# A four-engine selective-scan kernel: front steps in another order, folded kept blocks, and late sums moved behind products

## The chip, the cores and the metric

One Trainium2 chip, one core. The time is that of the device, in microseconds (us), for one launch of the whole program. TensorE is called PE in the profile, VectorE DVE, ScalarE ACT, GpSimd POOL, SyncE SP.

## The reference, cut to what matters

Four layers work on an image of 4 x 64 x 64 x 64 (batch, channels, height, width). Layer 1 is the one that the change touches. It runs the block below twice, over the columns and over the rows of the image, with 256 sequences of 64 steps each time.

```python
def selective_scan(u, delta, A, B, C, D):
    A = jnp.clip(A, -5.0, 5.0)
    dA = jnp.einsum('bld,dn->bldn', delta, A)
    dB_u = jnp.einsum('bld,bld,bln->bldn', delta, u, B)
    c = jnp.concatenate([dA[:, 1:], jnp.zeros_like(dA[:, :1])], axis=1)
    c = jnp.flip(c, axis=1)
    c = jnp.cumsum(c, axis=1)
    c = jnp.exp(jnp.minimum(c, 15.0))
    c = jnp.flip(c, axis=1)
    x = jnp.cumsum(dB_u * c, axis=1) / (c + 1e-06)
    y = jnp.einsum('bldn,bln->bld', x, C)
    return y + u * D

def mamba(x, in_w, conv_w, conv_b, xproj_w, dproj_w, dproj_b, A_log, Dp, out_w):
    x1, res = jnp.split(x @ in_w.T, 2, axis=-1)
    ...
    x1 = jax.nn.silu(jnp.transpose(xc, (0, 2, 1)))
    x_dbl = x1 @ xproj_w.T
    delta = jax.nn.softplus(x_dbl[..., :DTR] @ dproj_w.T + dproj_b)
    B = x_dbl[..., DTR:DTR + N]
    C = x_dbl[..., DTR + N:]
    y = selective_scan(x1, delta, A, B, C, Dp)
    return y * jax.nn.silu(res) @ out_w.T
```

The inner width d is 192 and there are 96 states n. So the scan is 96 times a cumulative sum over the steps, for each of 192 channels, and a weighted sum of all of them.

## The kernel before, in words

`build` runs six phases one after the other. The third and fourth are `phase_axis`, once with `vertical=True` (tiles with the prefix `h_`) and once without (`w_`). The other phases are not touched.

**Bodies.** `phase_axis` works on 64 bodies T, each of four sequences of 64 steps: two groups g, of two sequences each, whose 128 steps lie on the partitions in the scan. `bodies` gives every engine the same order of bodies, the first and the last few unrolled and the rest in a loop. Five instruction streams are written out by hand, one per engine, and meet at semaphores. Each engine takes its own stream strictly in order.

**Pairs and chunks.** The 96 states of both groups make 96 pairs P of states per body; 8 pairs are a chunk, so a body has 12 chunks. For a chunk:

- TensorE makes the exponents, three groups j of them (`fill`, into the PSUM tile `pe_e`), the third of a chunk at its predecessor's pairs 2 and 3.
- ScalarE turns each group into the factor c (`c_group`, into `cbuf`) and the weighted ratio 1/(c + 1e-6) (`r_group`, into `rbuf`), both as sigmoids. `cbuf` and `rbuf` have two halves, so a chunk's first group waits until the pairs of two chunks before are used up.
- The product of c and dx = delta * x is made by VectorE (`product`, into `xr`, 3 deep), with B folded in, in two instructions. For some pairs it is made without B: by POOL in place in `cbuf` (the list `OTHER`, 35 pairs), or by VectorE in one instruction (`WIDE`, 13 pairs). For these 48 pairs ScalarE makes a triangle scaled by B for each state (`triangles`, into `tb`, a ring of 6), 96 of them per body.
- TensorE multiplies by the triangle, which is the cumulative sum (`sums`, into `pz`, two banks), two pairs ahead.
- VectorE weights the result with C and the ratio (`weighted`).

**The sum over states.** Two pairs are a unit U (48 per body, 24 per group). `weighted` puts each unit in one of four places. The first kept unit of a group goes into `sm`, the other kept ones into `wr` (3 deep), and POOL adds them to `sm` (`add`). The first sent block of two units goes into `held` (8 slots, that is two halves of 4), the others into `sent` (2 deep), from where POOL issues a transfer that accumulates into `held` (`send`, 768 KB). At the end of a group POOL adds both halves of `held` to `sm` (`add_held`) and folds `sm` into `yb` (`tree`), at U = 34 for group 0 and U = 47, the last, for group 1 (`TREE_AT`). In POOL's stream the products of a unit stand before its additions, and the held additions and the tree stand after them.

**The front.** Between the pairs each engine does a step of the next body's front, and of the last body's end, all through one PSUM tile `pf`, whose uses are in a fixed order that `s_ff` (full) and `s_fe` (free) count: Y (y of the body before, turned), O (output projection), X (input projection and convolution), DT (step size), BC (B and C), Z (gate). Tables such as `X_SLOTS` say after which pair TensorE issues which matmul; ScalarE and VectorE take theirs at fixed chunks and pairs (`sig_x`, `parts`, `log`, `bc_copy`, `sig_z`, `piece1`, `piece2`, `out`; `make_xc` at pair 31, `prefix` at 54, `make_gate` at 58, `gated` at 12). `log` needs a table load before its logarithm and one after it. SP stores the suffix sum's three bf16 pieces and loads them in another layout (`feed`); TensorE waits for them at pair 84.

## Time and profile before

| | us |
|---|---|
| median of 3 runs | 18634.21 (18628.9 to 18642.46) |
| the profiled execution, its own time | 18637.84 |
| its span | 18636.1 |
| TensorE busy (matmuls) | 15693.2 (84%) |
| VectorE busy | 15893.3 (85%) |
| ScalarE busy | 15051.5 (81%) |
| POOL busy | 14571.3 (78%) |
| mean granted TensorE clock | 0.955 |

Busy time is the time in which an engine executes. A row of a timeline has the start, the length, the engine, the line, the tiles and the count of like instructions merged into it, and in brackets the idle time of the engine ahead of it and what ended it. Times are counted from the start of the span. A row of busy time by windows has the window, its length, then busy time (and count of instructions) of PE, PEld (its weight loads), DVE, ACT and POOL, the granted TensorE clock (1.00 is full speed), the share of the 16 DMA engines, and GB/s.

### The profile page before, as it was taken

To read this page: it belongs to the slowest core of one execution; us is meant where nothing else is said; L and a number is where in the kernel's file an instruction comes from. 1 tells how busy PE (TensorE), PEld (TensorE's weight loads), DVE (VectorE), ACT (ScalarE), POOL (GpSimd) and SP (SyncE) were. 2 spreads that over 40 slices of the span, in tenths; PEclk is the share of its full clock that TensorE was granted. 3 is DMA by queue.
4 is the path that set the end of the run, shared out by engine and by line. 5 is a ranking of instruction groups with operands and counts; after the bars stand their busy time and mean duration, and the time that the engine had idled before them with its cause. 6 is when DMAs were issued, how large, how long until landed. Compare 5 with 4: busy or idle time off the path is not lost. (4 is left out here: it accounts for less than half of the span.)

```text
span 18636.1 us, 316924 instructions
## 1 busy us (share of the span) xinstructions
PE 15693.2 (84%) x72568; PEld 10136.5 (54%) x72568; DVE 15893.3 (85%) x42315; ACT 15051.5 (81%) x26177; POOL 14571.3 (78%) x11848
## 2 busy tenths in 40 slices
PE   8878888888888888888788888888888888887788
PEld 3335555555555556555455555555555566654233
DVE  7998888888888888888888888888888888887799
ACT  7768888888888888888788888888888888885488
POOL 4668888888888888888688888888888888886577
PEclk9999999999999999999899999999999999999899
DMA  2013443444434444344344344444344443443000
GB/s 40 16 24 68 69 71 66 69 69 69 71 67 69 68 70 70 66 70 69 59 69 72 67 71 68 69 73 69 68 70 69 71 71 67 71 69 62 22 15 15
DMA packets 1109721, 1150.84 MB, mean 62 GB/s; under 512 B 915424, under 2 KB 934524, under 8 KB 1107836
## 3 DMA queue, kind: packets, MB, share of 16 engines
q0 software_dynamic: 165888, 906.04, 25.2%
q1 hardware_dynamic: 938596, 221.43, 10.6%
q8 instruction: 707, 11.58, 0.3%
q14 instruction: 1178, 9.65, 0.2%
q10 hardware_dynamic: 3352, 2.14, 0.1%
HBM read 152.05 MB, written 71.35 MB: 12 GB/s over the span
## 5 line engine op out<-in xcount | busy, mean ns | idle before, releaser
L1356 ACT ACTIVATE h_cbuf<-h_pe_e 128x1024 f32<-128x1024 f32 x2304 | 2361.0, 1025 | 1240.0 <-PE h_pz L1685 746.4
L1356 ACT ACTIVATE w_cbuf<-w_pe_e 128x1024 f32<-128x1024 f32 x2304 | 2360.9, 1025 | 1234.6 <-PE w_pz L1685 750.0
L1517 POOL TENSOR_TENSOR h_cbuf<-h_cbuf,h_dxs 128x384 f32<-128x384 f32 x2240 | 2500.6, 1121 | 1004.1 <-ACT h_cbuf L1356 967.9
L1517 POOL TENSOR_TENSOR w_cbuf<-w_cbuf,w_dxs 128x384 f32<-128x384 f32 x2240 | 2465.9, 1106 | 945.2 <-ACT w_cbuf L1356 899.5
L1495 POOL TENSOR_TENSOR h_sm<-h_sm,h_wr 128x768 f32<-128x768 f32 x1536 | 2951.8, 1922 | 294.2 <-DVE h_wr L1230 203.0
L1495 POOL TENSOR_TENSOR w_sm<-w_sm,w_wr 128x768 f32<-128x768 f32 x1536 | 2936.5, 1912 | 255.7 <-DVE w_wr L1230 200.9
L1689 PE MATMUL h_pz<-h_xr,h_tri 128*128 128x384 f32 x6144 | 2769.2, 533 | 427.2 <-DVE h_sent L1230 228.4
L1689 PE MATMUL w_pz<-w_xr,w_tri 128*128 128x384 f32 x6144 | 2764.6, 532 | 403.4 <-DVE w_sent L1230 227.0
L1230 DVE SCALAR_TENSOR_TENSOR h_wr<-h_pz,h_bct,h_rbuf 128x192 f32<-128x192 f32 x6144 | 2225.0, 410 | 511.0 <-PE h_pz L1685 325.4
L1230 DVE SCALAR_TENSOR_TENSOR w_wr<-w_pz,w_bct,w_rbuf 128x192 f32<-128x192 f32 x6144 | 2225.2, 410 | 472.9 <-PE w_pz L1685 330.6
L1685 PE MATMUL w_pz<-w_cbuf,w_tb 128*128 128x192 f32 x8960 | 1988.1, 347 | 498.1 <-POOL w_cbuf L1517 290.4
L1379 ACT ACTIVATE h_rbuf<-h_pe_e 128x1024 f32<-128x1024 f32 x2304 | 2364.7, 1026 | 37.0 <-DVE h_wr L1230 33.1
L1379 ACT ACTIVATE w_rbuf<-w_pe_e 128x1024 f32<-128x1024 f32 x2304 | 2364.8, 1026 | 35.1 <-DVE w_wr L1230 30.9
L1685 PE MATMUL h_pz<-h_cbuf,h_tb 128*128 128x192 f32 x8960 | 1982.2, 346 | 485.7 <-POOL h_cbuf L1517 264.8
L1178 DVE SCALAR_TENSOR_TENSOR w_xr<-w_cbuf,w_bct,w_pdx 128x192 f32<-128x192 f32 x6144 | 2239.0, 405 | 114.4 <-ACT w_cbuf L1356 102.9
L1178 DVE SCALAR_TENSOR_TENSOR h_xr<-h_cbuf,h_bct,h_pdx 128x192 f32<-128x192 f32 x6144 | 2238.7, 405 | 110.9 <-ACT h_cbuf L1356 101.2
L1371 ACT ACTIVATE w_tb<-w_tri,w_bct 128x128 f32<-128x128 f32 x6144 | 2052.8, 406 | 0.0
L1371 ACT ACTIVATE h_tb<-h_tri,h_bct 128x128 f32<-128x128 f32 x6144 | 2052.3, 406 | 0.0
L1668 PE MATMUL h_pe_e<-h_decay,h_lt 128*128 128x256 bf16 x9216 | 1828.0, 281 | 142.3 <-ACT h_rbuf L1379 89.0
L1668 PE MATMUL w_pe_e<-w_decay,w_lt 128*128 128x256 bf16 x9216 | 1827.5, 281 | 123.1 <-ACT w_rbuf L1379 89.0
L1685 PEld LDWEIGHTS w_pz<-w_cbuf,w_tb 128*128 128x128 f32 x8960 | 1500.6, 201 | 771.0 <-issue 543.3
L1685 PEld LDWEIGHTS h_pz<-h_cbuf,h_tb 128*128 128x128 f32 x8960 | 1494.9, 200 | 761.3 <-issue 532.7
(381 smaller groups left out, 30563.3 us busy)
## 6 DMA issues: line engine op xcount, KB each, us to landing
h_held<-h_sent POOLq DMA_DIRECT2D x576, 768.0 KB, 5.8
w_held<-w_sent POOLq DMA_DIRECT2D x576, 768.0 KB, 5.8
h_lt<-pieces_s SPq DMA_DIRECT2D x512, 96.0 KB, 6.4
w_lt<-pieces_s SPq DMA_DIRECT2D x512, 96.0 KB, 7.3
pieces_s<-h_pieces SPq DMA_DIRECT2D x384, 48.0 KB, 2.1
pieces_s<-w_pieces SPq DMA_DIRECT2D x384, 48.0 KB, 2.1
h_xt<-first_s SPq DMA_DIRECT2D x34, 128.0 KB, 9.0
w_xt<-first_s SPq DMA_DIRECT2D x34, 128.0 KB, 7.4
```

What stands on the lines that cost most here:

```text
L1178: ins = v.scalar_tensor_tensor(xr[:, P % 3, m * DX:(m + 1) * DX], cbuf[:, ch % 2, (n + m) % 16, :], bct[:, par, g * 2 * NX + n + m:g * 2 * ...
L1230: ins = v.scalar_tensor_tensor(place(g, u, (P % 2) * 2 + m), pz[:, P % 2, m * DX:(m + 1) * DX], bct[:, par, g * 2 * NX + NX + n + m:g * 2 ...
L1356: a.activation(cbuf[:, ch % 2, :, 64 * j:64 * j + 64].rearrange("p n (b d) -> p b n d", b=2), pe_e[:, G % 2 * 2:G % 2 * 2 + 2, :].rearrang ...
L1371: ins = a.activation(tb[:, i % RING, m, :], tri[:], ACT.Copy, scale=bct[:, q, g * 2 * NX + n + m:g * 2 * NX + n + m + 1])
L1379: a.activation(rbuf[:, ch % 2, :, 64 * j:64 * j + 64].rearrange("p n (b d) -> p b n d", b=2), pe_e[:, G % 2 * 2:G % 2 * 2 + 2, :].rearrang ...
L1495: tt(sm[:, g], sm[:, g], wr[:, RINGED.index((g, u)) % 3], ALU.add).then_inc(s_add, 1)
L1517: tt(c2, c2, dxs[:, g:g + 1, :].broadcast_to([128, 2, DX]), ALU.mult).then_inc(s_xo, 1)
L1668: mm = t.matmul(dst, lt[:, par, g * JQ + m, :], decay[:, m, n0:n0 + 16, :], start=True, stop=True)
L1685: mm = t.matmul(pz[:, P % 2, m * DX:(m + 1) * DX], tb[:, i % RING, m, :], x[:, m * DX:(m + 1) * DX], start=True, stop=True)
L1689: t.matmul(pz[:, P % 2, 0:2 * DX], tri[:], x, start=True, stop=True).then_inc(s_z, 1)
```

## The change

It does these things, in both axis phases:

- The uses of `pf` in a body come as X, DT, BC, Y, O, Z instead of Y, O, X, DT, BC, Z (`steps_of`), with new pairs and chunks for each. X now begins at pair 2, DT at 19, BC at 36, Y at 52, O at 59, Z at 75.
- `xc` has three buffers instead of two, taken by T mod 3.
- The second half of each group's `held` is added to its first half by a transfer of its own that accumulates (`send` with b = None, at U = 27 and U = 46), and `add_held` adds one half instead of two.
- `add_held` and `tree` have slots of their own: U = 33 and 36 for group 0, and U = 49 and 50, that is units 1 and 2 of the next body, for group 1.
- POOL's products stand one unit earlier (`LEAD = 8` where 7 was written out). Pair 35 leaves `OTHER` and pair 33 leaves `WIDE`, both become plain; pairs 2 and 82 join `WIDE`. That makes 34 pairs on POOL, 14 wide ones, and 48 scaled ones as before, so also 96 triangles.
- ScalarE takes the first two groups of a chunk, c and ratio, before any triangle, and has two places for triangles instead of three. Front steps stand after a chunk's last triangles.
- TensorE makes the third exponent group at a chunk's pairs 1 and 2 instead of 2 and 3.

```diff
-        xc = sb("xc", [128, 2, JB, TB])
+        xc = sb("xc", [128, 3, JB, TB])
...
-        Y_AT, O_AT, X_AT, DT_AT, BC_AT, Z_AT = 2, 3, 4, 5, 6, 7
-
-        Y_SLOTS = {8: (0, 1), 9: (2, 3), 10: (4,), 11: (5,)}
-        X_SLOTS = {20: (0,), 21: (1,), 22: (2,), 23: (3,), 24: (4, 5), 25: (6, 7), 26: (8,), 27: (9,), 28: (10,), 29: (11,)}
...
-        OTHER = [P for P in range(4, PAIRS) if P % 8 in (3, 5, 7)]
-        WIDE = [P for P in range(PAIRS) if P % 2 == 1 and P not in OTHER]
-        SCALED = [P for P in range(PAIRS) if P % 2 == 1]
+
+        def steps_of(first, last):
+
+            if first:
+                return dict(X=4, DT=5, BC=6, Z=7)
+            return dict(Y=2, O=3) if last else dict(X=2, DT=3, BC=4, Y=5, O=6, Z=7)
+
+        X_BIAS, DT_BIAS = 2, 19
+        X_SLOTS = {3: (0,), 4: (1,), 5: (2,), 6: (3,), 7: (4,), 8: (5,), 9: (6, 7), 10: (8, 9), 11: (10,), 12: (11,)}
+        DT_SLOTS = {20: (0, 1), 21: (2,), 22: (3,), 23: (4,), 24: (5,), 25: (6,), 26: (7,), 27: (8,)}
...
+        XS_CH, SX_CH, DT_CH, LOG_CH, BC_CH, P1_CH, P2_CH, O_CH, SZ_CH = 0, 1, 3, 3, 5, 5, 6, 8, 9
+        STEPS_U, SUFFIX_U, REST_U, PIECE_U, RESID_U = 17, 20, 25, 28, 37
+        XC_P, PREFIX_P, GATED_P, GATE_P = 17, 38, 57, 82
+        LESS, PLAIN, MORE = [35], [33], [3, 2, 82]
+        OTHER = [P for P in range(4, PAIRS) if P % 8 in (3, 5, 7) and P not in LESS]
+        WIDE = [P for P in range(PAIRS) if P % 8 == 1 and P not in PLAIN] + MORE
+        SCALED = sorted(OTHER + WIDE)
         NS2, RING = len(SCALED), 6
+        THIRD, LEAD = (1, 2), 8
...
-        TREE_AT = (34, 47)
+        FOLD_AT = ((1, 3), (1, 22))
+        HELD_AT, TREE_AT = (33, 49), (36, 50)
...
                         c_group(TT, nx, 0, free)
                         r_group(TT, nx, 0, free)
-                        triangles(TT, slot, nx, 0, ready, fresh)
                         c_group(TT, nx, 1, False)
                         r_group(TT, nx, 1, False)
-                        triangles(TT, slot, nx, 1, None, fresh)
...
+                        triangles(TT, slot, nx, 0, ready, fresh)
                         c_group(TT, nx, 2, False)
                         r_group(TT, nx, 2, False)
-                        triangles(TT, slot, nx, 2, None, fresh)
+                        triangles(TT, slot, nx, 1, None, fresh)
...
+                    src, dst = (held[:, g, 4:8], held[:, g, 0:4]) if b is None else \
+                        (sent[:, BLOCKS.index((g, b)) % 2], held[:, g])
...
-                    for n in range(2):
-                        pool.wait_ge(s_add, T * NA + NA + ahead("held", g, n))
-                        tt(sm[:, g], sm[:, g], held[:, g, 4 * n:4 * n + 4], ALU.add).then_inc(s_add, 1)
+                    pool.wait_ge(s_add, T * NA + NA + ahead("held", g, 0))
+                    tt(sm[:, g], sm[:, g], held[:, g, 0:4], ALU.add).then_inc(s_add, 1)
...
-                            if max((P - 7) // 2, 0) == U:
+                            if max((P - LEAD) // 2, 0) == U:
                                 product(T, P)
...
+                        if U + 2 * UN == HELD_AT[1] and not first:
+                            add_held(T - 1, 1)
+                        if U + 2 * UN == TREE_AT[1] and not first:
+                            tree(T - 1, 1)
```

First place: POOL at the end of a body and the start of the next. `h_sm<-h_sm,h_wr` is an addition, `h_sm<-h_sm,h_held` a held one, `h_sm<-h_sm` and `h_yb<-h_sm` are the tree, `h_cbuf<-h_cbuf,h_dxs` is a product; the branch is the loop. Before:

```order
L1495 TENSOR_TENSOR h_sm<-h_sm,h_wr 128x768 x4
L1508 TENSOR_TENSOR h_sm<-h_sm,h_held 128x768 x2
L1521 TENSOR_TENSOR h_sm<-h_sm 128x384
L1525 TENSOR_TENSOR h_yb<-h_sm 128x3x64
L942 UNCONDITIONAL_BRANCH
L942 ISA
L1515 ISA
L1517 TENSOR_TENSOR h_cbuf<-h_cbuf,h_dxs 128x384 x2
```

After:

```order
L1515 DMA h_held<-h_held 128x768
L1509 TENSOR_TENSOR h_sm<-h_sm,h_wr 128x768
L959 UNCONDITIONAL_BRANCH
L959 ISA
L1529 ISA
L1531 TENSOR_TENSOR h_cbuf<-h_cbuf,h_dxs 128x384 x2
L1529 REGISTER_ALU
L1531 TENSOR_TENSOR h_cbuf<-h_cbuf,h_dxs 128x384
L1520 ISA
L1521 ISA
L1522 TENSOR_TENSOR h_sm<-h_sm,h_held 128x768
L1531 TENSOR_TENSOR h_cbuf<-h_cbuf,h_dxs 128x384
```

Two held additions and the tree stood ahead of the next body's first products; now three products come first, and one held addition follows.

Second place: ScalarE around the log. `h_cbuf<-h_pe_e` is c, `h_rbuf<-h_pe_e` the ratio, `h_tb` a triangle, `h_ab` and `h_rl` belong to the step size. Before, at the end of the sixth chunk's turn:

```order
L1316 ACTIVATE h_ab<-h_pf 128x384
L1317 ACTIVATE h_rl<-h_pf 128x384
L1356 ACTIVATE h_cbuf<-h_pe_e 128x2x16x32
L1379 ACTIVATE h_rbuf<-h_pe_e 128x2x16x32
L1371 ACTIVATE h_tb<-h_tri,h_bct 128x128 x4
L1321 ACTIVATE h_ab<-h_ab 128x384
L1323 ACT_TABLE_LOAD
L1323 ACTIVATE h_ab<-h_ab 128x384
L1356 ACT_TABLE_LOAD
```

After, at the end of the fourth chunk's turn:

```order
L1388 ACTIVATE h_tb<-h_tri,h_bct 128x128 x2
L1373 ACTIVATE h_cbuf<-h_pe_e 128x2x16x32
L1396 ACTIVATE h_rbuf<-h_pe_e 128x2x16x32
L1388 ACTIVATE h_tb<-h_tri,h_bct 128x128 x2
L1333 ACTIVATE h_ab<-h_pf 128x384
L1334 ACTIVATE h_rl<-h_pf 128x384
L1338 ACTIVATE h_ab<-h_ab 128x384
L1340 ACT_TABLE_LOAD
L1340 ACTIVATE h_ab<-h_ab 128x384
L1373 ACT_TABLE_LOAD
```

The log stands two chunks earlier, right behind the steps that feed it, and after a chunk with four triangles instead of eight.

## Rows read from the trace of the kernel before

**Rows 1.** The page, part 1: busy time, share of the span, instructions.

```profile
PE 15693.2 (84%) x72568; PEld 10136.5 (54%) x72568; DVE 15893.3 (85%) x42315; ACT 15051.5 (81%) x26177; POOL 14571.3 (78%) x11848
```

**Rows 2.** VectorE's copy of dx (line 1188), once per body: ns min/median/max, first and last start.

```profile
L1188 DVE COPY h_dxs<-h_pdx x64: 547/550/554, 1340.5 to 9060.3; 128x384 f32<-128x384 f32 x64
L1188 DVE COPY w_dxs<-w_pdx x64: 547/550/554, 9286.0 to 16972.0; 128x384 f32<-128x384 f32 x64
```

**Rows 3.** Busy time by windows, one body's chunks 0, 3, 5, 6, 8, 9, 11 and the sum of all.

```profile
5012.95:5027.36 14.41, 8.97 (x36) 5.71 (x36) 8.91 (x27) 7.20 (x14) 11.46 (x11) 0.88 0.00 1
...
5045.81:5055.23 9.42, 9.37 (x60) 7.74 (x58) 8.96 (x27) 8.50 (x16) 7.31 (x7) 1.00 0.44 86
...
5064.78:5073.09 8.31, 8.31 (x46) 6.15 (x45) 8.31 (x26) 8.29 (x17) 7.09 (x7) 1.00 0.49 96
5073.09:5085.79 12.70, 9.38 (x54) 7.11 (x52) 9.56 (x27) 12.60 (x21) 8.85 (x9) 1.00 0.31 63
...
5094.52:5102.80 8.28, 7.73 (x38) 4.77 (x37) 8.28 (x26) 7.87 (x15) 7.75 (x7) 1.00 0.68 129
5102.80:5115.55 12.75, 9.00 (x38) 5.80 (x37) 8.53 (x26) 7.86 (x15) 12.43 (x11) 0.87 1.06 127
...
5123.84:5134.77 10.93, 8.88 (x45) 5.56 (x43) 8.93 (x27) 9.86 (x18) 10.70 (x9) 1.00 0.38 76
sum 121.82, PE 103.67 PEld 71.94 DVE 104.26 ACT 103.45 POOL 100.23; mean PE 8.64 PEld 6.00 DVE 8.69 ACT 8.62 POOL 8.35
```

**Rows 4.** The timeline at a body's boundary: POOL's sums and products, TensorE behind them.

```profile
5011.38 0.54 DVE L1172 TENSOR_TENSOR h_xr<-h_cbuf,h_pdx 128x384 f32<-128x384 f32 x1
...
5015.05 3.71 POOL L1508 TENSOR_TENSOR h_sm<-h_sm,h_held 128x768 f32<-128x768 f32 x2
...
5020.46 3.86 POOL L1517 TENSOR_TENSOR h_cbuf<-h_cbuf,h_dxs 128x384 f32<-128x384 f32 x4
5021.68 1.51 PE L1685 MATMUL h_pz<-h_cbuf,h_tb 128*128 128x192 f32 x4 [4.39 <-POOL h_cbuf L1517]
```

**Rows 5.** The timeline at group 0's sums, in chunk 9.

```profile
5102.86 4.01 POOL L1508 TENSOR_TENSOR h_sm<-h_sm,h_held 128x768 f32<-128x768 f32 x2
...
5108.54 1.27 ACT L1371 ACTIVATE h_tb<-h_tri,h_bct 128x128 f32<-128x128 f32 x4
5108.66 0.99 POOL L1517 TENSOR_TENSOR h_cbuf<-h_cbuf,h_dxs 128x384 f32<-128x384 f32 x1
...
5109.88 0.98 PE L1685 MATMUL h_pz<-h_cbuf,h_tb 128*128 128x192 f32 x4 [3.20 <-ACT h_tb L1371]
```

**Rows 6.** Busy time by windows, after each of the two stalls; columns as in rows 3.

```profile
5021.50:5025.00 3.50, 3.32 (x10) 2.25 (x11) 1.45 (x5) 0.00 (x0) 2.82 (x3) 0.55 0.00 0
5109.80:5114.20 4.40, 4.32 (x16) 3.14 (x17) 2.59 (x7) 0.01 (x1) 4.40 (x4) 0.61 1.38 111
```

**Rows 7.** The timeline around the log, and two waits behind it.

```profile
5068.18 0.51 ACT L1316 ACTIVATE h_ab<-h_pf 128x384 f32<-128x384 f32 x1
...
5070.78 0.82 PE L1685 MATMUL h_pz<-h_cbuf,h_tb 128*128 128x192 f32 x4
...
5071.90 0.57 ACT L1321 ACTIVATE h_ab<-h_ab 128x384 f32<-128x384 f32 x1
...
5075.62 1.02 ACT L1356 ACTIVATE h_cbuf<-h_pe_e 128x1024 f32<-128x1024 f32 x1
...
5077.62 0.39 PE L1668 MATMUL h_pe_e<-h_decay,h_lt 128*128 128x256 bf16 x2 [1.36 <-ACT h_rbuf L1379]
...
5081.87 0.74 DVE L1178 SCALAR_TENSOR_TENSOR h_xr<-h_cbuf,h_bct,h_pdx 128x192 f32<-128x192 f32 x2 [1.52 <-ACT h_cbuf L1356]
```

**Rows 8.** DMA issues of whole blocks (count, size, us to landing); POOL's time to issue one.

```profile
h_held<-h_sent POOLq DMA_DIRECT2D x576, 768.0 KB, 5.8
...
L1499 POOL DMA_DIRECT2D h_held<-h_sent x576: 814/864/1006, 1359.6 to 9164.6; - x192
```

**Rows 9.** The table of waits, POOL for ScalarE's factors: us in total, times, longest.

```profile
POOL h_cbuf L1517 <- ACT h_cbuf L1356: 967.9, 520, 5.3
```

More of the change, by code:

```diff
@@ L1249, in _ @@
                 dx_copy(0)
-                for T, par, half, first, last in bodies(dve):
-                    F, q = T + 1, 1 - par
+                for T, par, third, half, first, last in bodies(dve):
+                    F, q, x3, x1, f_at = T + 1, 1 - par, (third + 1) % 3, (third + 2) % 3, steps_of(first, last)
                     base = T * 6
@@ L1400, in _ @@
                     r_group(0, 0, j, False)
-                for part in CUTS[0:2]:
-                    triangles(0, 0, 0, part, 3, True)
+                triangles(0, 0, 0, 0, 3, True)
                 c_group(0, 0, 2, False)
                 r_group(0, 0, 2, False)
-                triangles(0, 0, 0, 2, None, True)
-                for T, par, half, first, last in bodies(act):
-                    F, q = T + 1, 1 - par
+                triangles(0, 0, 0, 1, None, True)
+                for T, par, third, half, first, last in bodies(act):
+                    F, q, x3, x1, f_at = T + 1, 1 - par, (third + 1) % 3, (third + 2) % 3, steps_of(first, last)
                     base = T * 6
@@ L1536, in _ @@
                 last.then_inc(s_dec, 1)
-                for T, par, half, first, last in bodies(pool):
-                    F, q = T + 1, 1 - par
+                for T, par, third, half, first, last in bodies(pool):
+                    F, q, x3, x1, f_at = T + 1, 1 - par, (third + 1) % 3, (third + 2) % 3, steps_of(first, last)
                     for U in range(48):
@@ L1708, in _ @@
                 sums(0, 1)
-                for T, par, half, first, last in bodies(pe):
-                    F, q = T + 1, 1 - par
+                for T, par, third, half, first, last in bodies(pe):
+                    F, q, x3, x1, f_at = T + 1, 1 - par, (third + 1) % 3, (third + 2) % 3, steps_of(first, last)
                     base = T * 6
```

176 lines of the change are left out of this document (91 added, 85 removed).

## The prediction, made before the changed kernel had run

> **What bounds the kernel now.** I read the page first. Four engines are busy for 78% to 85% of the span and the DMA engines far less [rows 1], so no engine is the bound by its sum, and I went on to the waits. The two axis phases hold nearly all the time: the copy of dx, once per body, runs 64 times in each, from 1340.5 to 9060.3 us and from 9286.0 to 16972.0 us, so a body takes (9060.3 - 1340.5)/63 = 122.5 us in the first and 122.0 us in the second [rows 2]. A body has 12 chunks of 8 pairs. I cut one body of 121.82 us into its chunks by VectorE's products [rows 3]. Chunks 5 and 8 take 8.3 us each with VectorE busy all through: that is the floor of a chunk. VectorE is busy 104.26 us of the 121.82 and idle 17.56, and the idle time stands in four places: chunk 0 (14.41 - 8.91 = 5.50), chunk 6 (3.14), chunk 9 (4.22) and chunk 11 (2.00). The other eight hold 2.7 us together.
>
> Who ends the waits in these places?
>
> - Chunk 0: POOL works off late additions, then adds the two halves of `held` (3.71 us), makes the tree (to 5020.46), and only then multiplies dx for the pairs that TensorE has been waiting for since 5017.3. TensorE is idle 4.39 us [rows 4].
> - Chunk 9: the same at the other group's end. Two halves take 4.01 us, the tree follows, the product starts at 5108.66 and ends at 5109.65, and TensorE goes on at 5109.88 after 3.20 idle us [rows 5]. The row names ScalarE's triangle, but its four triangles and POOL's product ended within 0.2 us of each other, and POOL's came behind 5.8 us of sums.
> - After both stalls the granted TensorE clock is 0.55 and 0.61 over 3.5 and 4.4 us, so part of that time at 1.2 GHz instead of 2.4 [rows 6]: a stall is followed by slow matmuls, which is in the chunk times above.
> - Chunk 6: ScalarE is busy 12.60 of 12.70 us [rows 3]. The log with its two table loads runs from 5071.90 to 5075.62, every later step comes late, TensorE waits 1.36 us for a ratio and VectorE 1.52 us for a decay factor [rows 7].
> - Chunk 11: POOL is busy 10.70 of 10.93 us, and VectorE waits for its ring of `wr`.
>
> **The change, part by part, per body.**
>
> 1. Late sums of group 1 move behind POOL's products of pairs 5, 7 and 11 of the next body. In the trace POOL ends its additions at 5015.05; with 0.86 us for one more transfer issued [rows 8] and a product of 1.0 us (3.86 for four [rows 4]), pair 5 is ready at 5016.9, before 5017.3. The 4.39 us go. What is late next is TensorE itself: the front's first projection now lies on chunks 0 and 1. In chunk 3, which holds 8 of its 12 matmuls now, TensorE is busy 9.37 of 9.42 us and VectorE idle 0.46. I leave 0.9 of chunk 0's 5.50: gain 4.6.
> 2. Sums of group 0: one half instead of two, behind the product of pair 75, and the tree three steps later. No product stands behind more than 1.9 us. Idle of 4.22 falls to 0.2: gain 4.0.
> 3. The log moves from the end of chunk 5's work to the end of chunk 3's, where chunk 4 has two scaled pairs fewer (4 triangles less, 1.27 us [rows 5]), the copy of B and C no longer stands between two groups, and sigmoids go ahead of triangles. Before, ScalarE began the next group at 5075.62, 4.0 us after TensorE had used up the buffer (5070.78 + 0.82) [rows 7]. Now I count 0.8 for abs and relu plus 3.7 for the log, less 1.3 of triangles and about 1 us of ScalarE's slack in the chunks ahead (0.9 in chunk 3 [rows 3]): some 2.2 us late, and the third group follows 0.6 us sooner. VectorE asks for it two or three pairs later than that. Chunk 6 keeps 0.5 of 3.14 (gain 2.6), and the new place is charged 0.5. Bounds: nothing, and all of the 3.1 again.
> 4. POOL sheds one held addition per group (2 of 1.9 us) and one product (1.0), and issues two transfers more (2 of 0.86). That is about 3.0 us less on a queue that overflows only in chunk 11; of its 2.00 us I take off 0.8.
> 5. Fold transfers: not in the trace. A whole block lands 5.8 us after issue [rows 8], so half a block takes between 0 and 5.8. Group 0's sum comes six steps after its fold (13 us), group 1's three steps and three products after it: nothing to at most 1 us of waiting on POOL, with no product needed soon behind it. I take 0, nearer the row, since 5.8 us are already spanned by one addition and three products (4.8 us).
> 6. VectorE: one wide product more (0.54 [rows 4]) and as many plain ones as before (48); 0.5 more, on the path.
> 7. The other steps keep their lengths and have cover: xc, prefix, gate and gated each follow their projection by at least two pairs (over 2 us). The third xc buffer lets y of the previous body be made at pair 52, after the next xc. The gate projection no longer waits for the copy of B and C. The pieces are ready at pair 57 instead of 65, so SP's stores and loads, done before pair 84 now, gain time. Front steps' waits left over: 0.3.
> 8. POOL asks for each chunk's product one step (two pairs) earlier, and TensorE makes the third exponent group one pair earlier. POOL will wait at most a pair longer per chunk with additions queued behind. It has a ring of three for that. I charge nothing in groups where only half the steps add.
>
> Sum for that body: 121.82 - 4.6 - 4.0 - 2.6 - 0.8 + 0.5 + 0.5 + 0.3 = 111.1 us. Mean bodies are 0.2 to 0.7 longer than this one, by the same boundary wait, and lose that too: 122.3 becomes 111.3, 11.0 less. There are 63 + 63 periods: 126 x 11.0 = 1386 us. The profiled execution took 18637.84 us (span 18636.1); it becomes 17,252. The median of the three runs, 18634.21, is 0.02% below it, so **17,250 us**.
>
> The Trainium skill, "DMA: Bandwidth & Descriptors", section on the anatomy of one SWDGE DMA, gives a fit of 2.0 us plus size over 436 KB per us. For the whole block it makes 3.8 us, where the trace has 5.8, so no run here supports its figure; for half a block it would make 2.9, an estimate that would leave the sum as it is.
>
> **Rivals.**
>
> - *Half of it.* The waits form again elsewhere: in chunk 0 TensorE, now with the projection and a fifth scaled pair, or POOL's tail, keeps 2.5 us, and the log costs its 3.1 us in chunk 4 as it did in chunk 6. For: four engines at 94% in a shorter body (ScalarE 103.45 of 111) leave little to catch up with. The body is 111.3 + 5.6 = 116.9, the time 17,250 + 126 x 5.6 = 17,960. Chance 0.24.
> - *POOL blocks at the head of its queue* (slower). Part 8 goes wrong: POOL already waits 967.9/64 = 15.1 us per body for ScalarE's factors in 520 waits [rows 9]. Its work after the change is 100.2 - 3.0 = 97.2 us, so the change is slower than before once POOL's waits pass 122.3 - 97.2 = 25.1 us. If each of 12 waits grows by a pair (1.3 us), they are 30.7: a body of 127.9, or 18,638 + 126 x 5.6 = 19,340 us. Against it: the factor's exponents come a pair earlier too. Chance 0.05.
> - *VectorE decides.* If VectorE's own work, the highest in a body, set the pace and the waits were only its shadow, taking work from POOL would be worth nothing and the wide product would cost 0.54 x 128 = 69 us: 18,700, slower by 0.4%. Against it: VectorE is idle in those very chunks. Chance 0.03. The Trainium skill, "Perfetto Trace Analysis", section on identifying the most-contended engine, says to optimize the engine of highest occupancy first; that rule speaks against this change, which relieves the least busy of the four. The rows disagree with it here, as it looks at averages and they at chunks.
> - *It doesn't do what it says.* POOL reaches the moved sums so late that the next products stand behind them as before: no change, about 18,640. Chance 0.03.
> - *More.* The small waits of chunks 1 to 4 shrink too, a body of 108: 16,830. Chance 0.07.
>
> **How the numbers follow.** The forecast has 0.58. Its own range is 16,950 to 17,650, from the charges above between nothing and three of them doubled. The range for 8 in 10 takes in most of the first and of the last rival, each with a few hundred us of spread about its own figure: 16,850 to 18,050. Faster by over 0.2% (about what a measurement of this kernel can tell from no change): 0.58 + 0.24 + 0.07 = 0.89; within it 0.03; slower 0.05 + 0.03 = 0.08.
>
> **What would show it.** Right: periods between copies of dx near 111 us; no TensorE idle above 1 us on POOL's product; no clock below 1.00 in the middle of a body; chunks 0, 6 and 9 under 10 us; ScalarE without idle time in chunks 3 to 6, VectorE waiting under 1 us after the log. Part 3 is wrong if chunk 4 or 5 takes over 12 us; part 8 if POOL's waits for factors pass 20 us per body or VectorE waits for `sm`; part 5 if POOL waits for the fold over 1 us per body. The forecast is wrong if a body stays above 115 us.

## The result, and the profile after

| | before | after |
|---|---|---|
| median, us | 18638.33 (18628.9 to 18650.15, 4 runs) | 17350.32 (17346.37 to 17366.98, 4 runs) |
| the profiled execution, us | 18637.84 | 17346.37 |
| mean granted TensorE clock | 0.955 | 0.978 |

The ratio is 0.931 (0.9294 to 0.9326): 1288 us or 6.9% faster, 100 us slower than the 17,250 forecast and inside the range. The span is 17344.5 us. Its busy line, which answers to [rows 1]:

```profile
PE 15345.0 (88%) x72568; PEld 9862.9 (57%) x72568; DVE 15921.2 (92%) x42443; ACT 15021.8 (87%) x26177; POOL 14270.5 (82%) x11720
```

VectorE and ScalarE do as much work as before, and POOL 301 us less. For VectorE the 1288 us came out of idle time; TensorE's busy time fell by 348 us as well, at a higher granted clock. VectorE's copy of dx, now line 1205, gives the length of a body, as [rows 2] did:

```profile
L1205 DVE COPY h_dxs<-h_pdx x64: 549/551/554, 1342.7 to 8385.7; 128x384 f32<-128x384 f32 x64
L1205 DVE COPY w_dxs<-w_pdx x64: 549/551/554, 8600.8 to 15688.2; 128x384 f32<-128x384 f32 x64
```

That is 111.8 us in the first phase (122.5 before) and 112.5 in the second (122.0): 63 x 10.7 + 63 x 9.5 = 1273 us of the 1288.

One body of the changed kernel in windows, cut and read as [rows 3]; chunks 0, 3, 4, 6, 8, 9, 11 and the sum of all twelve:

```profile
4587.75:4597.31 9.56, 8.94 (x49) 6.25 (x48) 8.82 (x27) 7.34 (x14) 9.48 (x10) 1.00 0.23 41
...
4615.51:4624.21 8.70, 8.53 (x50) 6.40 (x48) 8.56 (x27) 8.51 (x14) 6.12 (x6) 1.00 0.41 82
4624.21:4635.41 11.20, 8.74 (x41) 5.33 (x40) 10.01 (x30) 10.74 (x18) 8.83 (x8) 1.00 0.36 70
...
4644.34:4652.62 8.28, 7.73 (x43) 5.48 (x42) 8.28 (x26) 8.28 (x16) 8.28 (x9) 1.00 0.48 95
...
4661.80:4670.08 8.28, 7.73 (x38) 4.77 (x37) 8.28 (x26) 8.28 (x16) 6.97 (x6) 1.00 0.93 121
4670.08:4679.57 9.49, 8.32 (x45) 5.74 (x43) 8.19 (x26) 9.49 (x19) 8.24 (x8) 1.00 1.15 167
...
4688.30:4698.49 10.19, 8.59 (x45) 5.57 (x43) 8.84 (x27) 9.59 (x19) 9.96 (x8) 1.00 0.40 79
sum 110.74, PE 100.81 PEld 69.69 DVE 104.27 ACT 102.35 POOL 97.37; mean PE 8.40 PEld 5.81 DVE 8.69 ACT 8.53 POOL 8.11
```

VectorE is busy 104.27 us here and was busy 104.26 before; its idle time fell from 17.56 to 6.47. Chunks 0, 6 and 9 lost 4.9, 4.4 and 3.3 us. The clock is 1.00 throughout.

The boundary of two bodies, which answers to [rows 4] (a timeline):

```profile
4588.34 2.12 POOL L1509 TENSOR_TENSOR h_sm<-h_sm,h_wr 128x768 f32<-128x768 f32 x1
...
4590.12 3.20 POOL L1531 TENSOR_TENSOR h_cbuf<-h_cbuf,h_dxs 128x384 f32<-128x384 f32 x3
...
4592.63 0.92 PE L1705 MATMUL h_pz<-h_cbuf,h_tb 128*128 128x192 f32 x4
...
4592.99 2.10 POOL L1522 TENSOR_TENSOR h_sm<-h_sm,h_held 128x768 f32<-128x768 f32 x1
```

POOL makes three products first, and TensorE takes the first of them at 4592.63 with no wait. The held addition follows at 4592.99, and TensorE waits for none of the products behind it. Before, TensorE was idle 4.39 us in this place. The clock no longer falls here either.

What is left, in the table of waits (us in total, times, longest):

```profile
POOL h_cbuf L1531 <- ACT h_cbuf L1373: 700.3, 510, 4.9
...
PE h_pe_e L1688 <- ACT h_rbuf L1396: 110.5, 66, 2.1
...
POOL h_sm L1509 <- DMA h_held<-h_sent: 96.9, 104, 2.8
...
DVE h_wr L1247 <- POOL h_sm L1509: 75.9, 114, 1.6
...
DVE h_sent L1247 <- DMA h_held<-h_sent: 55.3, 30, 2.9
```

POOL's wait for factors is 10.9 us per body (15.1 before, [rows 9]). TensorE waits 1.7 us per body for a ratio: that is the log, in its new place. POOL's wait for the accumulating transfers is 1.5 us per body in this phase (1.0 before: 66.6 us in 31 waits). VectorE's, 0.9 us per body, is new.

The log's new place, body 29 of the first phase (timeline, answers to [rows 7]):

```profile
4622.49 1.28 ACT L1340 ACT_TABLE_LOAD   x1
...
4624.33 1.28 ACT L1373 ACT_TABLE_LOAD   x1
...
4627.62 0.39 PE L1688 MATMUL h_pe_e<-h_decay,h_lt 128*128 128x256 bf16 x2 [1.70 <-ACT h_rbuf L1396]
...
4627.85 0.86 PE L1709 MATMUL h_pz<-h_xr,h_tri 128*128 128x384 f32 x2
...
4628.74 0.74 DVE L1247 SCALAR_TENSOR_TENSOR h_sent<-h_pz,h_bct,h_rbuf 128x192 f32<-128x192 f32 x2 [1.19 <-PE h_pz L1709]
```

And the same place one body later:

```profile
4738.36 0.61 PE L1688 MATMUL h_pe_e<-h_decay,h_lt 128*128 128x256 bf16 x2 [1.70 <-ACT h_rbuf L1396]
...
4738.77 1.49 PE L1709 MATMUL h_pz<-h_xr,h_tri 128*128 128x384 f32 x2
...
4740.29 0.74 DVE L1247 SCALAR_TENSOR_TENSOR h_sent<-h_pz,h_bct,h_rbuf 128x192 f32<-128x192 f32 x2 [2.00 <-PE h_pz L1709]
```

TensorE waits 1.70 us in both, but then the same two matmuls take 0.86 us in one and 1.49 in the other. Windows of 3.5 us from the end of the wait have a reason in the clock column: 1.00 for the first body, 0.55, mostly 1.2 GHz, for the second.

```profile
4627.60:4631.10 3.50, 3.32 (x15) 1.96 (x16) 2.36 (x8) 3.50 (x6) 1.14 (x2) 1.00 0.15 28
4738.36:4741.86 3.50, 3.50 (x10) 2.11 (x11) 1.42 (x5) 3.50 (x6) 1.05 (x2) 0.55 0.15 28
```

But the slow matmuls are not all of it. Chunk 4 as a whole, in the second of these bodies (the first, 11.20 us, is above):

```profile
4734.96:4748.05 13.09, 9.94 (x41) 6.19 (x40) 10.95 (x30) 10.97 (x18) 10.36 (x10) 0.87 0.42 83
```

Of the 1.89 us that it is longer, 0.94 is busy time of VectorE. The suffix sum's scan (`prefix`), one instruction per body, makes nearly all of that. First body, then second:

```profile
4630.96 1.97 POOL L1531 TENSOR_TENSOR h_cbuf<-h_cbuf,h_dxs 128x384 f32<-128x384 f32 x2 [2.29 <-ACT h_cbuf L1373]
...
4632.65 1.09 DVE L1166 TENSOR_TENSOR_SCAN h_sf<-h_mask,h_rl 128x384 f32<-128x384 f32 x1
```

```profile
4743.75 1.81 POOL L1509 TENSOR_TENSOR h_sm<-h_sm,h_wr 128x768 f32<-128x768 f32 x1
...
4744.43 1.95 DVE L1166 TENSOR_TENSOR_SCAN h_sf<-h_mask,h_rl 128x384 f32<-128x384 f32 x1
```

In both, the scan ends 0.81 us after the end of the POOL instruction that ran when it started (4632.93 and 4633.74; 4745.56 and 4746.38). In all traces together 1387 of these scans start beside a POOL instruction, and 1385 of them end 0.81 to 0.82 us after its end. Before, where POOL did nothing at that time, the scan took 0.95 us. So the new order put the scan beside POOL's work: it takes 1.24 us on average in the first phase and 1.35 in the second, by what is left of the POOL instruction that runs when it starts. I read this as the scan standing still until then.

So chunk 4 has two lengths, 11.2 and about 13.0 us. Of the 63 bodies with a log, 15 are long in the first phase and 27 in the second, and these are the bodies with the low clock and with a long scan (1.71 us on average; 1.09 in the others). That difference is 12 x 1.8 = 22 us, of the 76 us (63 x 1.2) that the second phase gained less. Of the rest, chunk 11 has about 66 and chunk 10 about 25, and chunk 0 gained 35 more in the second phase.

### The profile page after: what moved, and what is told of

Same layout as the page of the kernel before. It is cut to its first block and busy times, and to the rows that moved or that the text cites. A ratio compares the mean times of both kernels' runs of the same rounds, so it can differ in the third digit from the quotient of the medians.

```text
span 17344.5 us, 317054 instructions
## 1 busy us (share of the span) xinstructions
PE 15345.0 (88%) x72568; PEld 9862.9 (57%) x72568; DVE 15921.2 (92%) x42443; ACT 15021.8 (87%) x26177; POOL 14270.5 (82%) x11720
## 5 line engine op out<-in xcount | busy, mean ns | idle before, releaser
L1509 POOL TENSOR_TENSOR w_sm<-w_sm,w_wr 128x768 f32<-128x768 f32 x1536 | 2992.2, 1948 | 152.9 <-DVE w_wr L1247 86.1
L1709 PE MATMUL h_pz<-h_xr,h_tri 128*128 128x384 f32 x6144 | 2710.9, 523 | 369.2 <-DVE h_sent L1247 166.6
L1531 POOL TENSOR_TENSOR w_cbuf<-w_cbuf,w_dxs 128x384 f32<-128x384 f32 x2176 | 2369.0, 1124 | 763.2 <-ACT w_cbuf L1373 739.3
L1531 POOL TENSOR_TENSOR h_cbuf<-h_cbuf,h_dxs 128x384 f32<-128x384 f32 x2176 | 2367.0, 1126 | 725.4 <-ACT h_cbuf L1373 700.3
L1247 DVE SCALAR_TENSOR_TENSOR h_wr<-h_pz,h_bct,h_rbuf 128x192 f32<-128x192 f32 x6144 | 2208.0, 411 | 135.5 <-POOL h_sm L1509 75.9
L1388 ACT ACTIVATE h_tb<-h_tri,h_bct 128x128 f32<-128x128 f32 x6144 | 1977.6, 408 | 0.0
L1388 ACT ACTIVATE w_tb<-w_tri,w_bct 128x128 f32<-128x128 f32 x6144 | 1976.6, 407 | 0.0
L1247 DVE SCALAR_TENSOR_TENSOR w_sent<-w_pz,w_bct,w_rbuf 128x192 f32<-128x192 f32 x4608 | 1642.4, 411 | 235.9 <-PE w_pz L1709 91.9
L1247 DVE SCALAR_TENSOR_TENSOR h_sent<-h_pz,h_bct,h_rbuf 128x192 f32<-128x192 f32 x4608 | 1642.4, 411 | 223.7 <-PE h_pz L1709 83.2
L686 POOL TENSOR_TENSOR m_gv<-m_hs,m_cv 128x512 f32<-128x512 f32 x1024 | 1321.9, 1302 | 624.1 <-DVE m_hs L512 576.1
L1705 PE MATMUL h_pz<-h_cbuf,h_tb 128*128 128x192 f32 x8704 | 1820.6, 332 | 11.5 <-DVE h_sent L1247 11.2
```

What stands on the lines that cost most here:

```text
L686: tt(gv[:, n % GV, :], hs[:, n, :], cv[:, n % CV, :], ALU.mult).then_inc(s_g, 1)
L1247: ins = v.scalar_tensor_tensor(place(g, u, (P % 2) * 2 + m), pz[:, P % 2, m * DX:(m + 1) * DX], bct[:, par, g * 2 * NX + NX + n + m:g * 2 ...
L1388: ins = a.activation(tb[:, i % RING, m, :], tri[:], ACT.Copy, scale=bct[:, q, g * 2 * NX + n + m:g * 2 * NX + n + m + 1])
L1509: tt(sm[:, g], sm[:, g], wr[:, RINGED.index((g, u)) % 3], ALU.add).then_inc(s_add, 1)
L1531: tt(c2, c2, dxs[:, g:g + 1, :].broadcast_to([128, 2, DX]), ALU.mult).then_inc(s_xo, 1)
L1705: mm = t.matmul(pz[:, P % 2, m * DX:(m + 1) * DX], tb[:, i % RING, m, :], x[:, m * DX:(m + 1) * DX], start=True, stop=True)
```

## The experiments

Each kernel ran beside the kernel before on one chip (18616 to 18646 us; medians 18626.58, 18625.53 and 18628.96 for the three groups of four). The changed kernel was not run again with them: its time goes with 18638.33 for the kernel before, so a difference of some 12 us between it and one of these says nothing. Mean chunk lengths over 52 bodies (9 to 60) of the first phase, in us, from the starts of VectorE's weightings of each chunk's first pair; the chunks left out stay within 0.8 us of the changed kernel's:

```
kernel                                median us   ch 0   ch 4   ch 6   ch 9  ch 10  ch 11   body
before                                 18638.33  14.81   9.55  12.70  12.91   8.72  10.81 122.67
after                                  17350.32  10.20  11.57   8.29   9.13   8.84  10.53 111.85
e1_both_sums_back                      18564.97  15.15  12.07   8.28  14.17   8.93   9.64 121.56
e2_sums_back_lead8                     18222.51  15.37  11.19   8.28   9.92   8.89  11.48 118.46
e3_no_fold                             17518.71  10.21  11.82   8.28  10.19   9.18  10.78 113.75
e4_only_sums_moved                     17926.55   9.12  10.09  12.69  10.23  10.34  11.77 117.47
e5_after_no_log_table                  17193.81  10.07  10.65   8.28   9.09   8.87  10.43 110.67
e6_before_no_log_table                 18292.08  14.85   9.55  10.00  12.74   8.78  10.86 119.96
e7_old_number_of_wide_products         17678.17  10.00  14.23   8.28   9.25   8.85  10.74 114.45
e8_third_sent_buffer                   17338.85  10.11  11.71   8.29   8.10   8.77  11.66 111.92
e9_wide_products_back_no_log_table     17105.88  10.04   9.82   8.29   9.29   9.01  10.61 110.16
e10_products_one_unit_later            17425.75  10.29  12.32   8.29   8.70   8.91  10.85 112.64
e11_triangles_ahead_of_sigmoids        17413.79  10.11  11.91   8.29   9.56   9.02  10.50 112.67
e12_two_more_products_on_POOL          17330.85  10.31  11.60   8.29   9.64   9.21  10.36 112.04
```

**POOL's sums, the fold and the lead.** Four kernels took these apart. The first two are the changed kernel with POOL's sums in the old slots and no fold:

```diff
-        HELD_AT, TREE_AT = (33, 49), (36, 50)
+        HELD_AT, TREE_AT = (34, 47), (34, 47)
...
-            CARRIER[FOLD_AT[g]] = (g, None)
```

The first has `LEAD = 7` beside it, the second keeps 8.

> The changed kernel with three of its parts undone on POOL: no fold (two halves of held are added again), the held additions and the tree back at units 34 and 47 of the same body, and the products one unit later again (LEAD = 7). Theory A (POOL's sums ahead of products make the two stalls, 4.6 and 4.0 us of a body): both stalls return, a body of 112.1 + 8.6 = 120.7 us, the time 17350 + 126 x 8.6 = 18430 us, between 18250 and 18600; TensorE waits over 3 us once at a body's start and once in chunk 9, and the clock falls behind both. Theory B (the front's new order and the log's new place bring most of the gain): under 17800 us.

> As the run before, but with the products one unit earlier kept (LEAD = 8). Theory A, told more closely: the stall at a body's start returns whole (pairs 5 and 7 stand at unit 0 in either case), that in chunk 9 only in part, since pair 77's product now stands ahead of the sums and pair 79's, due two pairs later, behind them: about 1.6 of 3.2 us. A body of 112.1 + 4.6 + 2 = 118.7 us, the time about 18180 us, 200 to 350 under the run before. Rival: the earlier products cost POOL more waiting for ScalarE's factors with additions queued behind, and this run is not faster than the run before.

Measured: 18564.97 (ratio 0.9967, 0.9954 to 0.9979) and 18222.51 (0.9783, 0.9767 to 0.9799). The first lies in its range, the second 40 us above the forecast: theory A, in which the rest of the change gives little while POOL's sums stand where they did. Everything but the slots, the fold and the lead is worth 62 us. Chunk 6 did lose 4.4 us in the first of them, but chunk 4 took 2.5 and chunk 9 1.3. I read chunk 9 as a stall of POOL's queue that grows when the work around it shrinks; no run shows that by itself. TensorE waited for POOL's product in both, first kernel first (table of waits):

```profile
PE h_pz L1699 <- POOL h_cbuf L1531: 432.8, 122, 5.4
```

```profile
PE h_pz L1699 <- POOL h_cbuf L1531: 296.9, 118, 4.8
```

In the changed kernel TensorE's matmuls have no such row; only their weight loads keep one, of 4.0 us in all. The lead alone makes 342 us here: it puts the product of pair 77 ahead of group 0's sums, and chunk 9 falls from 14.17 to 9.92. Chunk 4 falls too, from 12.07 to 11.19: the scan takes 1.89 us on average in the first kernel and 1.08 in the second, as it now starts at the end of a POOL product instead of beside an addition. Chunk 11 takes 1.8 back.

The third kernel keeps the new slots and undoes the fold alone: both halves of `held` are added by POOL.

```diff
-            CARRIER[FOLD_AT[g]] = (g, None)
...
-                    SUMS.append(("held", g, 0))
+                    SUMS += [("held", g, 0), ("held", g, 1)]
```

> The changed kernel without the two fold transfers; POOL adds both halves of held, in the changed kernel's slots. POOL has 2 x 1.85 more and 2 x 0.87 less, about 2 us per body. Theory C (the fold is worth little, since POOL had 14 us of idle time in a body, and its transfer delays the chain of accumulating transfers, for which VectorE waits 0.9 us and POOL 1.1 us per body): between 17250 and 17350 us, and VectorE's waits for held transfers nearly gone. Theory D (POOL's load at the boundary is what counts): 1 to 2 us per body more, 17480 to 17600 us.

Measured: 17518.71 (0.9406, 0.939 to 0.9421), in the range of theory D (17,480 to 17,600) and not in mine, theory C (17,250 to 17,350). The fold is worth 168 us, by chunk 9 in the first phase (1.1 us) and by chunk 11 in the second (12.93 against 11.15), where chunk 4 falls (11.19 against 12.00), since not one of its bodies is long. Against the kernel with the sums back and the same lead it shows the slots alone: 18222.51 - 17518.71 = 704 us.

The fourth goes the other way, the kernel before with the new slots and nothing else (group 0's held additions stay at U = 34, as there is no fold and no lead):

```diff
-        TREE_AT = (34, 47)
+        HELD_AT, TREE_AT = (34, 49), (36, 50)
```

> The kernel before with one part alone: the held additions (both halves) and the tree of group 1 at units 1 and 2 of the next body, the tree of group 0 at unit 36 instead of 34. Everything else as before. Theory A: the stall at a body's start goes (4.6 us), that in chunk 9 shrinks but 3.7 us of held additions still stand ahead of pair 77 (1 to 2.5 us gained), and chunk 6 keeps its 3.1 us of idle time. The turn of y, at pairs 8 to 11, may now wait for the tree, by up to 1.5 us. Gain 4.5 to 7 us per body, 17760 to 18070 us. Theory B: under 2 us per body, over 18400 us.

Measured: 17926.55 (0.9623, 0.9607 to 0.9639), a gain of 700 us, inside theory A's 17,760 to 18,070. The slots give 700 first and 704 late in the chain, but that the two agree so well is in part luck. Late, nearly all of it is chunk 0 (15.37 to 10.21), since the lead has cleared chunk 9. First, chunk 0 gives 5.7 and chunk 9 2.7, and chunks 4, 10 and 11 take 3.1 back. Step by step from before to after: 62 (front order, log, product lists, sigmoids), 342 (lead), 704 (slots), 168 (fold), together 1276 of 1288 us.

**The log.** Its logarithm becomes a copy, so that both table loads go, in the changed kernel and in the one before:

```diff
-                    a.activation(ab[:], ab[:], ACT.Ln).then_inc(s_ln, 1)
+                    a.activation(ab[:], ab[:], ACT.Copy, scale=-0.5).then_inc(s_ln, 1)
```

> The changed kernel with ScalarE's logarithm (of the factors' product, once per body) replaced by a copy scaled by -0.5, so that no function table is loaded for it and the other table is not loaded back; the values of the gate's log part are not the reference's. Everything else stands where the changed kernel has it. Theory A (the log's new place costs what the trace of the changed kernel shows there: TensorE waits 1.7 us per body for ScalarE's factors and VectorE then about 1.2 to 1.4 us for TensorE's product): 1.2 to 1.9 us per body go, about 17,170 us (17,100 to 17,230), and chunk 4 falls from 11.6 to about 10. Rival (the wait is only handed on, since POOL or the transfers behind it are late as well): no change, 17,330 to 17,370 us.

> The kernel before with the same replacement, the log standing in its old place; the gate's log part is again not the reference's. Theory A (VectorE's idle time in chunk 6, 12.7 us against 8.3 to 9.6 in plain chunks, is the wait behind the log and its two table loads): about 2.6 to 3.1 us per body go, 18,250 to 18,310 us, and chunk 6 falls to about 9.8. Rival (chunk 6 is long because of what VectorE itself has to do there, or POOL's part follows at once with its own wait): under 100 us gained. Beside the run with the table loads gone from the changed kernel, the difference tells how much of the log's cost the move itself had removed.

Measured: 17193.81 (0.9231, 0.9218 to 0.9244), 157 us less than the changed kernel, and 18292.08 (0.9817, 0.9804 to 0.9831), 334 us less than before. The loads cost 2.7 us per body in the old place, all in chunk 6, and still 0.9 in chunk 4 of the first phase and 1.4 in that of the second (12.00 against 10.64). Both times lie in theory A's ranges, against rivals that saw the wait only handed on; chunk 4 was to fall to about 10 and stayed at 10.65. VectorE's idle time there goes from 1.41 (second phase 1.66) to 0. The chunk gains less, because VectorE now starts its scan 0.8 us into POOL's addition: it takes 1.82 us in every body instead of 1.24 and 1.35 on average. So the scan takes back 0.6 and 0.5 us per body of what the edit saves.

**The product lists.** The next kernel sets them back, and another does so without the table loads:

```diff
-        LESS, PLAIN, MORE = [35], [33], [3, 2, 82]
+        LESS, PLAIN, MORE = [], [], [3]
```

> The changed kernel with the lists of pairs whose product VectorE takes set back: POOL gets the plain number of products again and VectorE fewer wide ones (the lists LESS and PLAIN empty, MORE with the one pair that the new order needs). Theory A (POOL was only an engine that others wait for at a few places, and there LEAD 8 covers it): the POOL work that comes back, about 3 us per body, costs 0.5 to 1 us per body, 17,410 to 17,480 us. Rival (VectorE at 0.54 us less per body decides, since it is busy 92% of the span): 17,280 us or less. Second rival (POOL decides): 3 us per body more, 17,700 us.

> The changed kernel with both edits that were tried singly: the old number of wide and POOL products (LESS and PLAIN empty, MORE with one pair) and ScalarE's logarithm replaced by a copy scaled by -0.5, so that no table is loaded (the gate's log part is not the reference's). Putting the products back alone cost 328 us, all of it in chunk 4; taking the table loads out alone gained 157. Theory A (the two scaled pairs taken out of chunk 4 are worth something only because the log stands there: it and their four triangles are one queue on ScalarE): without the table loads the products cost little, 17,190 to 17,290 us, chunk 4 near 10.9. Rival (POOL's or ScalarE's load by itself makes chunk 4 long): 17,480 to 17,540, chunk 4 near 13.3.

Measured: 17678.17 (0.9487, 0.9474 to 0.95), 328 us more than the changed kernel; without the loads 17105.88 (0.9184, 0.917 to 0.9198), 88 us *less* than with the new lists. It is not for POOL's load that the new lists are worth 328 us. They clear pairs 33 and 35 for the log, and without its table loads they come out as a loss. The timeline behind the log, lists back:

```profile
4706.59 0.39 PE L1688 MATMUL h_pe_e<-h_decay,h_lt 128*128 128x256 bf16 x2 [3.04 <-ACT h_rbuf L1396]
...
4708.53 0.74 DVE L1247 SCALAR_TENSOR_TENSOR h_sent<-h_pz,h_bct,h_rbuf 128x192 f32<-128x192 f32 x2 [4.00 <-PE h_pz L1705]
```

and the window of 3.5 us from the end of that wait:

```profile
4706.59:4710.09 3.50, 3.50 (x11) 2.51 (x12) 1.39 (x4) 3.49 (x6) 0.50 (x2) 0.55 0.01 0
```

The wait is 3.04 us instead of 1.70. Where 15 of 63 chunks were long with 1.70, none is short now: 7 take 12.5 us and 56 take 14.3 to 14.9. The two pairs that went back cost 2.7 us in chunk 4, of which 1.34 us are TensorE's longer wait. VectorE's idle time there grows by 2.8 us, and the slow matmuls behind the wait (a low clock in 56 of 63 bodies against 15) are most of the rest. The scan adds 0.4 (1.66 on average). Of my figures for the kernel with the lists back, theory A's (17,410 to 17,480) and the first rival's fell, and 17,678 is near the second rival's 17,700. But its reason falls with the kernel that has no loads: POOL has the same load there, and nothing is lost. That kernel came out under even theory A's range (17,190 to 17,290). It does so mainly by the scan, not by the lists' own work. Chunk 4 takes 9.82 us against 10.65, and the scan, which starts at the end of a POOL product here and beside an addition there, 1.01 against 1.82 on average: 0.81 of the 0.83 us. Pair 35's plain product spares VectorE 0.7 more, and new idle time (0.57 against 0) takes most of that back.

**A third `sent` buffer.** The room comes from the tensor of ones, which gave the bias its moving operand.

```diff
-        sent = sb("sent", [128, 2, 8, DX])
+        sent = sb("sent", [128, 3, 8, DX])
```

> The changed kernel with three buffers in place of two for the halves that are sent to the held block, so that VectorE waits for the accumulating transfer three blocks back; the room comes from dropping the tensor of ones, whose matmul reads the identity broadcast in its place. Theory A (the 0.9 us per body that VectorE waits for these transfers, 55 us in the first half and 63 us in the second, were on the path): about 17,240 us (17,200 to 17,290). Rival (the transfers into one held block follow one another anyhow and POOL waits for the last of them at its sum, so the wait only moves to POOL and from it to VectorE's next stop): 17,320 to 17,370 us.

Measured: 17338.85 (0.9307, 0.9294 to 0.9319), in the rival's range and no different from the changed kernel. VectorE's wait did go: chunk 9 fell from 9.13 to 8.10. Chunk 11 rose from 10.53 to 11.66. Both in one body (windows):

```profile
4672.30:4680.40 8.10, 7.72 (x43) 5.44 (x42) 8.10 (x26) 8.10 (x17) 7.93 (x8) 1.00 0.96 159
...
4689.13:4701.72 12.59, 8.61 (x45) 5.55 (x43) 8.90 (x27) 9.55 (x19) 10.83 (x8) 1.00 0.32 64
```

VectorE's wait for POOL's additions to free `wr` doubles, from the 75.9 us above:

```profile
DVE h_wr L1245 <- POOL h_sm L1507: 146.5, 152, 2.7
```

That wait takes back in chunk 11 what chunk 9 gave.

**The lead, the triangles, and two more products on POOL.** Three kernels, each the changed one with one edit. `LEAD = 7`:

> The changed kernel with POOL's products one unit later in its queue (LEAD 7 for 8), everything else as changed. With the late sums in their old slots this same edit made 342 us. Theory A (the lead only matters where a long piece of sums stands ahead of a product; with the sums moved there is none, and POOL waits less at the head of its queue): 17,330 to 17,480 us. Rival (the lead is worth the same anywhere, since TensorE comes to POOL's product in every chunk with nothing to spare): 17,650 to 17,720 us.

Measured: 17425.75 (0.9355, 0.9342 to 0.9368), 75 us more and in theory A's range, where the same edit made 342 with the sums in the way. The 75 us are mostly the scan again, and not a wait for a product: it starts beside POOL's addition in every body (1.79 us on average instead of 1.24 and 1.35), and chunk 4 takes 12.0 us even where the clock is 1.00, against 11.2. POOL's wait for factors falls from 10.9 to 4.7 us per body without the lead: six microseconds of waiting at the head of its queue are cheap as long as what stands behind is not urgent.

The triangles between the sigmoids again:

```diff
-        CUTS = (0, 1)
+        CUTS = (0, 1, 2)
...
+                        triangles(TT, slot, nx, 0, ready, fresh)
                         c_group(TT, nx, 1, False)
                         r_group(TT, nx, 1, False)
-                        triangles(TT, slot, nx, 0, ready, fresh)
+                        triangles(TT, slot, nx, 1, None, fresh)
...
-                        triangles(TT, slot, nx, 1, None, fresh)
+                        triangles(TT, slot, nx, 2, None, fresh)
```

> The changed kernel with ScalarE's triangles in their old places between the sigmoids of a chunk (the first after the first group, the second after the second), everything else as changed. Theory A (ScalarE has at most 1 us of slack in most chunks, and behind the log and at the group's boundary what it delivers late is the decay factor that VectorE multiplies by, not the triangle): 0.5 to 1.5 us per body more, 17,400 to 17,540 us, in chunks 4, 5 and 0. Rival (triangle or sigmoid, TensorE needs both at nearly the same pair, and the order is worth nothing): 17,330 to 17,370 us.

Measured: 17413.79 (0.9345, 0.9332 to 0.9357), 63 us more, in the first phase in chunks 4 and 9 (0.3 and 0.4 us), in the second in chunk 11 (0.5), and not in 5 or 0: the size was right, two of the three places weren't. Nor is the reason shown. In chunk 4 TensorE waits less than before (1.43 us for 1.70), and the scan takes more (mostly 1.52 us for 1.09).

Pairs 49 and 65 from VectorE's wide products to POOL:

```diff
+        OTHER, WIDE = sorted(OTHER + [49, 65]), [P for P in WIDE if P not in (49, 65)]
```

> The changed kernel with the wide products of pairs 49 and 65 made by POOL in place of VectorE (pair 49 in chunk 6, pair 65 in chunk 8, the two chunks in which VectorE has no idle time and POOL 0.8 and 1.3 us). VectorE has 2 x 0.54 us less to do per body, POOL 2 x 1.0 us more. Theory A (once the long stalls are gone VectorE sets the length of these two chunks, and POOL reads the sums in time): about 1 us per body less, 17,220 to 17,290 us, chunks 6 and 8 at 7.8 each. Rival (POOL's sums come later by as much and VectorE then waits for its ring, in these or the next chunks): 17,340 to 17,550 us.

Measured: 17330.85 (17303.17 to 17334.77; 0.9299, 0.9287 to 0.9312). That is 19 us under the changed kernel, with overlapping intervals, so no difference is shown, and it lies in neither range. The products lay one chunk ahead of where I had looked for them: chunk 5 fell to 8.48 and chunk 7 to 8.95. In the first phase chunks 9 and 10 gave 0.9 us back, as VectorE's wait for room in `sent` grew from 55.3 to 90.0 us; in the second phase it did not, and the body kept 0.5 us. Taking work from the busiest engine (92%) gave next to nothing. No kernel that computes the whole beats the changed one by more than that.

## Why the prediction was right, and where not

- **Part 1** (late sums of group 1, gain 4.6 in chunk 0): right. 14.81 to 10.20 us in the first phase, 4.6, and 5.2 in the second. The slots run as the arithmetic of [rows 4] had it, and both slot experiments confirm the cause.
- **Part 2** (group 0's sums, gain 4.0 in chunk 9): the size was right (12.91 to 9.13, 3.8), the reason half wrong. I made much of standing behind the product of pair 75, but the sums stood behind that one before as well. The product that came late was that of 77, and the lead of part 8, charged at nothing, clears it by itself (14.17 to 9.92). So do slots and fold without the lead (8.70), and with both the second adds little.
- **Part 3** (log, gain 2.6, new place charged 0.5): the gain came, VectorE's idle time in chunk 6 fell from 3.13 to 0. The charge was mis-sized: the loads cost 0.9 in the first phase and 1.4 in the second. Even at full clock VectorE waits 1.19 us behind the log, and I left out what [rows 6] had shown of stalls, that slow matmuls follow. In the sum it hardly shows, which is luck: 1.09 us of idle time of the old chunk 4 (TensorE late for its pairs) went with the new order, and in VectorE's idle time the chunk lost only 0.3 and 0.6 on balance. The fewer triangles were counted here as 1.3 us, and are worth 2.7, mostly for the same reason.
- **Part 4** (lighter POOL, gain 0.8 in chunk 11): the term that failed. Chunk 11 changed by -0.3 in the first phase and +0.8 in the second (10.38 to 11.15). The product shed gave 0.2 there; the addition shed with the fold gave 168 us, in chunk 9 in one phase and in 11 in the other.
- **Part 5** (fold 0): right as for POOL, whose held addition waited for a fold once per phase, 1.3 us. I had not asked who else waits for that queue: VectorE now waits 0.9 us per body for room in `sent`. That is not the fold's doing, since without it the wait is 122.3 us in the first phase against 55.3.
- **Part 6** (VectorE + 0.54): 0.2 on balance, since its busy sum rose by 27.9 us over 128 bodies; in the body shown by nothing. The longer scans are in that sum, so the rest took less; why stays open.
- **Part 7** (0.3 left over): chunks 1 to 3 have 0.97 us of VectorE's idle time together, against 1.59 before, but chunks 5 and 7, which had none, have 0.58 and 0.35. "The other steps keep their lengths" is wrong for the scan: 0.95 us before, 1.24 and 1.35 now.
- **Part 8** (nothing): worth a gain of 0.6 us per body as the last edit, for a reason I had not seen (the scan), and 2.7 before the slots. POOL's waits per body stayed at 10.9, far from the 25.1 at which its rival decides.

The sum was 11.0 us per body; measured are 10.7 and 9.5, 0.9 too few on average, 126 x 0.9 = 113 us. Measured in VectorE's idle time, mean of both phases, chunk 11 fell short by 1.1 us, chunk 9 by 0.5, and chunks 5 and 7 have 0.9 of new idle time where I had 0.3 left over. Against that chunk 6 gave 0.5 more, chunks 1 to 3 gave 0.6, and part 6 cost 0.3 less. These leave 0.8 of the 0.9. That the forecast came within 100 us is thus owed to parts 1 and 2, which were right in size, and to smaller terms that offset each other.

Of the rivals, *half of it* named the log as what could remain. With the old lists the table loads cost more than its 3.1 us in chunk 4 (4.4, 14.23 against 9.82), so the lists kept it away. *VectorE decides* fell: POOL's sums gave most of the gain. The rule in the Trainium skill, "Perfetto Trace Analysis", section on identifying the most-contended engine, would now send one to VectorE at 92%; the kernel that took two wide products from it shows no difference. *More* stays out: no body took less than 109.4 us.

The marks I set: periods near 111, no wait on POOL's product, chunks 6 and 9 under 10 us on average and no wait for the fold held. Chunk 0 missed by 0.2 in the first phase (10.20; 9.83 in the second). ScalarE was to have no idle time in chunks 3 to 6; it has 0.46 us in chunk 4 of the body shown. "No clock below 1.00 in mid body" and "VectorE waits under 1 us after the log" failed (0.55; 1.19 to 2.00 us), and chunk 4 passes 12 us in 42 of 126 bodies: part 3's own mark for being wrong, and it was.

## What to carry over

Where engines take their queues in order, look for what stands *ahead* of an urgent instruction, not for the busiest engine: moving the late sums of POOL, the least busy of four, gave some 700 us whether done first or late, while relief of VectorE and a third buffer gave nothing that can be told. Price a TensorE stall with the slow matmuls behind it, not with the wait alone, and expect an edit's worth to depend on what else is there: one unit of lead was worth 342 us before the sums moved and 75 after. When a step moves, look at what will run beside it: the same scan took 0.95 us in its old place and 1.0 to 1.9 us in its new one, by what POOL was doing.
